# A transformer block on one core: odd halves scaled on ScalarE with an adding transfer, expert tiles in the place of filler transposes, odd gates one term later

## What is computed

```python
x = x + layernorm(attn(layernorm(x)))          # attn(x) = x + ripple(x)
x = x + layernorm(ffn(layernorm(x)))

# ripple: 8 heads of 16; tokens 0,1,2,4,...,512 back
w    = softmax(q . k[t - off] / 4)             # 11 terms
tele = sum_off w[off] * v[t - off]
conv = depthwise causal convolution of v, 7 taps
low  = (fq @ (fk^T v)) / (fq . sum fk)         # fq, fk = elu(.) + 1
out  = (tele + conv + low) @ Wo

# ffn: 8 experts of 64 hidden units, top 2 of them, and one shared expert
scores = sigmoid(x @ gate_W) * route_scale     # top 2, normalised
y = sum_e gate[e] * (gelu(x @ W1[e] + b1[e]) @ W2[e] + b2[e])
y = y + gelu(x @ Ws1 + bs1) @ Ws2 + bs2
```

## Time and profile before

| | |
|---|---|
| median of 3 runs | 289.01 us (288.4 to 289.19) |
| profiled execution | 289.32 us, span of the trace 287.3 us |
| PE busy | 251.7 us, 88% of the span |
| DVE busy | 233.3 us, 81% |
| ACT busy | 194.9 us, 68% |
| POOL busy | 92.9 us, 32% |
| granted TensorE clock, mean | 0.978 |

### The profile page before, as it was taken

One profiled execution on the slowest core, in us unless ns is written; L12 is line 12 of the kernel. 1 busy time (PEld: TensorE's weight loads), 2 busy tenths in 40 slices (PEclk: granted clock), 3 DMA queues, 4 the chain that ended last, 5 costly groups with the idle time before them and its releaser, 6 DMA issues.

```text
span 287.3 us, 4891 instructions
## 1 busy us (share of the span) xinstructions
PE 251.7 (88%) x1670; PEld 179.6 (63%) x1670; DVE 233.3 (81%) x614; ACT 194.9 (68%) x449; POOL 92.9 (32%) x150
## 2 busy tenths in 40 slices
PE   5965995988798889999988999999989799999993
PEld 5422693786644567787645576797636587785383
DVE  6499789478997869789978969789779989957933
ACT  2383466814979957777899956867798655557841
POOL 5920252114374213217092213117043114331003
PEclk9997997999799999999999999999999999999998
DMA  6508999600279984330479973300699955100012
GB/s 199 134 26 240 222 218 196 127 0 2 71 232 234 220 177 84 65 82 2 136 244 215 238 150 73 73 5 0 193 219 219 214 137 109 40 0 1 0 39 73
DMA packets 24258, 35.27 MB, mean 123 GB/s; under 512 B 4053, under 2 KB 17198, under 8 KB 24234
## 3 DMA queue, kind: packets, MB, share of 16 engines
q1 hardware_dynamic: 20346, 21.59, 26.6%
q0 software_dynamic: 3888, 13.37, 25.0%
HBM read 5.07 MB, written 2.10 MB: 25 GB/s over the span
## 4 chain that ended last, share of the span: by engine, by line
PE 50%; ACT 21%; DVE 18%; POOL 5%; issue 4%; POOLq 0%; DVEq 0%; ACTq 0%
PE psH L1413 11%; PE psF L1475 7%; DVE prods L286 7%; PE psY L1515 6%; PE psA L1319 4%; PE psA L1381 4%; ACT xn L610 3%; PE psA L1515 2%; POOL rstd L491 2%; ACT squares L723 2%; ACT xn L730 2%; PE psG L1501 2%; DVE prods L1048 2%; PE psA L1311 2%; PE psH L1410 2%
## 5 line engine op out<-in xcount | busy, mean ns | idle before, releaser
L286 DVE TENSOR_TENSOR prods<-qT,kT 128x1024 f32<-128x1024 f32 (+1 forms) x48 | 50.5, 1109 | 4.4 <-POOL neg_half L454 2.8
L1413 PE MATMUL psH<-ident,prods 128*128 128x128 f32 x324 | 39.9, 273 | 0.0
L491 POOL TENSOR_TENSOR rstd<-var,neg_half 128x4 f32<-128x4 f32 (+2 forms) x27 | 37.2, 1378 | 2.2
L1413 PEld LDWEIGHTS psH<-ident,prods 128*128 128x128 f32 x324 | 36.4, 141 | 2.3 <-issue 2.3
L489 POOL TENSOR_SCALAR var<-ss 128x4 f32<-128x4 f32 (+1 forms) x24 | 8.2, 343 | 90.7 <-ACT squares L778 39.2
L1048 DVE TENSOR_TENSOR prods<-v_shift,prob 128x896 f32<-128x896 f32 x32 | 34.7, 1083 | 0.0
L1475 PE MATMUL psF<-x3T,w 128*128 128x512 f32 x58 | 29.4, 614 | 1.4 <-ACT hid L754 1.4
L1381 PE MATMUL psA<-prods,slot_sel 128*32 128x512 f32 x168 | 24.1, 624 | 5.4 <-DVE kv L988 2.3
L1048 DVE TENSOR_TENSOR prods<-v_tok,prob 128x128 f32<-128x128 f32 (+2 forms) x60 | 20.9, 370 | 3.5 <-PE psH L1413 3.3
L754 ACT ACTIVATE hid<-psF,b1c 128x512 f32<-128x512 f32 x29 | 19.1, 688 | 6.6 <-PE psF L1475 6.6
L1191 DVE TENSOR_TENSOR hid<-hid,psG 128x512 f32<-128x512 f32 x30 | 19.3, 681 | 3.3 <-PE psG L1501 3.3
(11 more groups left out here) (253 smaller groups left out, 591.7 us busy)
## 6 DMA issues: line engine op xcount, KB each, us to landing
v_shift<-v_tok SPq DMA_DIRECT2D x20, 448.0 KB
convT<-tapT POOLq DMA_DIRECT2D x8, 512.0 KB, 6.2
x_res<-L_attn_x SPq DMA_DIRECT2D x4, 512.0 KB, 9.4
tapT<-tapT POOLq DMA_DIRECT2D x4, 512.0 KB, 11.5
out<-y_out SPq DMA_DIRECT2D x7, 256.0 KB, 2.3
x_in<-L_attn_x SPq DMA_DIRECT2D x3, 512.0 KB, 4.1
v_shift<-v_tok SPq DMA_DIRECT2D x4, 384.0 KB
convT<-kexp POOLq DMA_DIRECT2D x3, 512.0 KB, 9.5
```

The lines of the kernel that those rows point to most:

```text
L286: return eng.tensor_tensor(prods[:, QUADS * (s % 2) + q, t0:t1], qT[:, t0:t1], kT[:, PRE - off + t0:PRE - off + t1], ALU.mult)
L491: return nc.gpsimd.tensor_tensor(rstd[:, cols], var[:, cols], neg_half[:, cols], ALU.pow)
L1413: ins = pe.matmul(dst, terms[:, j % TERM_BUFS, m, :], ident[:], is_transpose=True, start=False, stop=(m == live[-1]))
```

## The change

It has these parts, all in passes 1 to 3 (the end in pass 4 keeps its order):

1. Odd units 1 and 3 go the even units' way: `scale_outputs(u0 - 1)` at the start of ACT's pass and `add_residual(u0 - 1)` on POOL, ahead of `ln1`. DVE's `finish` for them goes. `residual` of the odd half waits for the landing of that transfer.
2. All of these units' outputs lie in one bank, `psG[:, 0]`, no longer the even ones in `psY`. PE's waits move with it: `output` and `experts_out` each lose one, and `spread_gates` waits for the scaling.
3. PE: the first two tiles of `experts_out(u0)` stand where 18 filler transposes were, ahead of `turn_x3(u1)` and of the next batch's K projection; the other two stand between the steps of the front of u1; K follows them. The 14 fillers ahead of `output(b, 1)` give way to one tile of u1 (pass 0 keeps them), and the last tile of u1 no longer stands in the next pass. In pass 3 one of two groups of 12 fillers goes.
4. DVE: six gate steps of u0 stand ahead of `residual(u1)`; `weigh_low` follows the second pair of `gate_hidden` (its reciprocal stays ahead); the 24 gate steps of u1 stand in j = 2 to 4, up to three in a place, where they were in j = 1 to 4, two in a place.
5. ACT: the taps come later by one, and tap 6 stands behind `evacuate_x3(u1)`; `normalise3(u1)` stands ahead of the evacuation of the transposed next batch; `norm4` of the odd unit follows fk's evacuation.
6. POOL: of the last two tap additions, that of tap 6 comes last.

```diff
         def outputs(u):
             if u < 2 * B - 3:
-                return psG[:, 0, :] if u % 2 else psY[:]
+                return psG[:, 0, :]
             return psY[:] if u == 2 * B - 1 else psA[:, u % 2, :]
...
             def sum_taps_third(b):
-                pool.wait_ge(tap_scaled, upto(b - 1, TAPS, 7))
                 pool.wait_ge(sums_added, N_DMA * upto(b - 1, N_SUMS, 2))
-                add_tap(b, 0, 6, sums_added)
-                pool.wait_ge(sums_added, N_DMA * upto(b - 1, N_SUMS, 3))
                 pool.wait_ge(side_added, N_DMA * upto(b - 1, N_SIDE, 2))
                 add_tap(b, 0, 2, sums_added)
+                pool.wait_ge(tap_scaled, upto(b - 1, TAPS, 7))
+                pool.wait_ge(sums_added, N_DMA * upto(b - 1, N_SUMS, 3))
+                add_tap(b, 0, 6, sums_added)
...
-                tiles = slice(0, TPH)
-                pool.wait_ge(out_scaled, u // 2 + 1)
-                nc.gpsimd.dma_start(y_out[:, tiles, :], x2[:, tiles, :], accum_op=ALU.add).then_inc(x2_added, N_DMA)
+                tiles = slice(u % 2 * TPH, (u % 2 + 1) * TPH)
+                pool.wait_ge(out_scaled[u % 2], u // 2 + 1)
+                nc.gpsimd.dma_start(y_out[:, tiles, :], x2[:, tiles, :],
+                                    accum_op=ALU.add).then_inc(x2_added[u % 2], N_DMA)
...
                 if attn:
+                    if b >= 2:
+                        ln4(u0 - 1)
+                        add_residual(u0 - 1)
                     if more:
                         ln1(b + 1)
-                    if b >= 2:
-                        ln4(u0 - 1)
...
                 if attn:
+                    if b >= 2:
+                        scale_outputs(u0 - 1)
                     if ffn:
                         gate_logits(u0)
-                        scale_taps(b, range(4, TAPS))
+                        scale_taps(b, range(3, 6))
...
+                    if ffn:
+                        normalise3(u1)
                     if more:
                         evacuate_x(b + 1)
                     if ffn:
-                        normalise3(u1)
                         evacuate_x3(u1)
+                        scale_taps(b, range(6, TAPS))
                         evacuate_shared(u1)
                         gate_logits(u1)
...
                         evacuate_x3(2 * b)
-                        scale_taps(b + 1, range(1, 2))
                         token_major_fk(b + 1)
-                        evacuate_shared(2 * b)
-                        scale_taps(b + 1, range(2, 3))
                         if ffn:
                             norm4(u1)
-                        scale_taps(b + 1, range(3, 4))
+                        evacuate_shared(2 * b)
+                        scale_taps(b + 1, range(1, 3))
...
                 dve.wait_ge(x_res_ld, upto(b, N_DMA, 16))
                 dve.wait_ge(ln2_ready, u + 1)
                 if 0 < b < B - 1 and half:
-                    dve.wait_ge(out_ready[1], upto(b, TPH, 0))
+                    dve.wait_ge(x2_added[1], upto(b, N_DMA, 0))
                 elif 0 < b < B - 1:
-                    dve.wait_ge(x2_added, upto(b, N_DMA, 0))
+                    dve.wait_ge(x2_added[0], upto(b, N_DMA, 0))
...
-                    if b >= 2:
-                        finish(u0 - 1)
                     if ffn:
+                        gates(u0, range(4, 10))
                         residual(u1)
-                        gates(u0, range(4, 24))
+                        gates(u0, range(10, 24))
                     softmax_logits(b)
                     if ffn:
                         gate_hidden(u0, range(0, 2))
-                    weigh_low(b)
+                    invert_low()
                     if ffn:
                         gate_hidden(u0, range(2, 4))
+                    weigh_low(b)
                     softmax_weights(b)
                     for j in range(NT):
-                        def two_gate_steps(n):
-
-                            if ffn and 1 <= j <= TPH:
-                                gates(u1, range(2 * (3 * (j - 1) + n), 2 * (3 * (j - 1) + n + 1)))
-
-                        weigh(b, j, two_gate_steps)
+                        def three_gate_steps(n):
+
+                            if ffn and 2 <= j <= TPH:
+                                first = 3 * (3 * (j - 2) + n)
+                                gates(u1, range(min(first, N_GATE_STEPS), min(first + 3, N_GATE_STEPS)))
+
+                        weigh(b, j, three_gate_steps)
                         if ffn:
...
             def output(b, half):
                 pe.wait_ge(hT_ready, upto(b, 2, half + 1))
-                if b and not half:
-                    pe.wait_ge(out_scaled, b)
...
                     if c == 0 and u % 2 == 0 and 0 < u < 2 * B - 2:
-                        pe.wait_ge(out_ready[1], upto(u // 2, TPH, 0))
+                        pe.wait_ge(out_scaled[1], u // 2)
+                    elif c == 0 and u % 2 and u < 2 * B - 1:
+                        pe.wait_ge(out_scaled[0], u // 2 + 1)
...
             def experts_out(u, tiles=range(TPH)):
                 if u >= 2 * B - 3:
                     pe.wait_ge(scores_read, 2 * B)
-                elif u % 2 == 0:
-                    pe.wait_ge(low_used, u // 2 + 2)
...
                     if ffn:
                         turn_logits(u0)
-                        if b >= 2:
-                            experts_out(u0 - 1, range(TPH - 1, TPH))
...
                     if ffn:
                         spread_gates(u0, range(2, 4))
-                    if more and ffn:
-                        pe.wait_ge(hidden_free, upto(u1, N_HIDDEN, -1))
-                        keep_busy(FILL_K, front(u1, X3))
+                    if ffn:
+                        pe.wait_ge(gated, upto(u0, 4, 4))
+                        experts_out(u0, range(0, 2))
+                        turn_x3(u1)
+                        experts_out(u0, (2,))
+                        gate_logits(u1)
+                        experts_out(u0, (3,))
+                        turn_logits(u1)
                     if more:
                         project_k(b + 1)
-                    else:
-                        keep_busy(FILL_LAST, psA[:, 0, :])
                     if ffn:
-                        turn_x3(u1)
-                        experts_out(u0, (0,))
-                        gate_logits(u1)
-                        experts_out(u0, (1,))
-                        turn_logits(u1)
-                        experts_out(u0, range(2, TPH))
...
                     if more:
                         if ffn:
                             pe.wait_ge(gated, upto(u1, 4, 4))
-                        keep_busy(FILL_OUT, psG[:, 1, :])
+                            experts_out(u1, (0,))
+                        else:
+                            keep_busy(FILL_OUT, psG[:, 1, :])
...
                         project_v(b + 1)
                         if ffn:
-                            experts_out(u1, range(0, 2))
+                            experts_out(u1, range(1, 3))
                         token_major_v(b + 1)
                         turn_x3(2 * b)
                         if ffn:
-                            experts_out(u1, range(2, 3))
+                            experts_out(u1, (3,))
```

More of the change, by code:

```diff
@@ L51 @@
 FILL_FRONT = 5
-FILL_LAST, FILL_K, FILL_OUT = 12, 18, 14
+FILL_LAST, FILL_OUT = 12, 14
 CH = 5
@@ L783, in scale_outputs @@
                 if u >= 2:
-                    act.wait_ge(out_stored[0], upto(u // 2, N_DMA, 0))
+                    act.wait_ge(out_stored[u % 2], upto(u // 2, N_DMA, 0))
                 act.wait_ge(ln4_ready, u + 1)
-                for j in range(TPH):
-                    last = nc.scalar.activation(y_out[:, j, :], outputs(u)[:, bass.ts(j, P)], ACT.Copy,
+                for n, j in enumerate(unit_tiles(u)):
+                    last = nc.scalar.activation(y_out[:, j, :], outputs(u)[:, bass.ts(n, P)], ACT.Copy,
                                                 scale=rstd4[:, j:j + 1])
-                last.then_inc(out_scaled, 1)
+                last.then_inc(out_scaled[u % 2], 1)
             first_normalise()
```

16 lines of the change are left out of this document (8 added, 8 removed).

## The result

The changed kernel takes 291.45 us (median of 9 runs, 290.67 to 293.52), the kernel before 289.17 us (288.17 to 290.48, 9 runs) beside it. The ratio is 1.010, 95% interval 1.007 to 1.013: slower by 0.7 to 1.3%, where 0.9% faster was forecast. The time lies above the predicted range. Some executions took over 1.5% longer than the fastest of the same kernel (295.9 us against 288.68 with the odd half finished on DVE); all medians and ratios here leave them out, and one kernel whose profiled execution was of that kind is left out of the table of lengths.

A forecast was written before the change was run, and what follows sets the result against it. A chain nearly all ACT, then PE until the terms' end, was taken to bound each pass. Terms -1.3 - 0.3 - 1.3 + 0.8 - 0.5 = -2.6 us gave 286.4 us from 289.01; range 283.9 to 289.3 us.

The forecast's parts named there:

- is it kept?: Whether PE's 1.3 us lasts until the terms end: PE stays the bound and passes it on.
- PE's stretch: Passes 1 and 2, from K to the terms' end: hidden of u1 starts earlier, 1.3 us saved in each.
- Pass 2, first norm: ACT's stretch: first norm of batch 3, waiting for `ln1`, starts at 149.2, not 149.5 us: 0.3 us saved.
- Landing: Odd half's adding transfer lands in 5.5 us, bounds 3.3 and 9: nothing lost in pass 2, 0.8 us in pass 3.
- Rival 1: Odd half's landing is slow, deciding point 7.0 us; at 9 us the time is 293.0 us. Chance 0.13.
- Pass 3 after the exponential: Tiles replace fillers; PE could save up to 2 us, DVE allows 0.59 less 0.2: 0.5 us saved.
- The tap sums are also needed at `add_conv`; they have some us of room in pass 1: In PE's stretch, tap sums were taken not to hold up `add_conv`, so the 1.3 us is kept.
- rival 3: PE's 1.3 us given back as taps' sum, Gelu or second gates set `add_conv`: 288.4 us. Chance 0.10.
- if `add_conv` waits for the taps' sum: One of three signs, in the profile after, that would show the prediction wrong.
- rival 4: PE's clock falls; without fillers the new gap is 1.1 us, in pass 3 about 1.4. Chance 0.05.

The follow-up runs named there:

- late taps, old order: Changed kernel with the last two tap additions in their former order and, in pass 3, the first pair issued behind `ln3(u1)`: 288.36 us, ratio 0.999.
- gap filled: Kernel of "late taps, old order" plus 16 PE fillers in pass 3 where PE waits for the odd half's landing: 286.09 us, ratio 0.9919.
- fastest version: Kernel of "late taps, old order" with the odd half finished on VectorE, no odd adding transfer: 286.1 us, ratio 0.9905; run again 285.54 us, 0.9892.
- late taps alone: Changed kernel with only the first pair of tap additions of pass 3 moved behind `ln3(u1)` on POOL: 291.2 us, ratio 1.0089.

## Why the prediction was wrong

The working of single steps held; the question "is it kept?" did not.

- **PE's stretch**, forecast 1.3 us saved each pass: 1.47 us in pass 1 (41.37 to 39.90 in all kernels with the old tap order) and in pass 2 of the changed kernel (41.39 to 39.92, with `add_conv` waiting for PE). Right.
- **Pass 2, first norm**, forecast 0.3 saved: against the start of the half it began at 19.65 us and not 20.03 (147.42 - 127.77; 149.50 - 129.47), 0.4 saved. Right. `ln1` took 3.0 us, forecast 3.2. The squares behind the norm then waited 0.93 us for the landing, which I had at nothing, so the odd half as a whole lost 0.67 us.
- **Landing**, taken as 5.5 us: 6.11 and 5.7 us. Pass 3's odd half lost 1.06 us, forecast 0.8. Right. Rival 1 (slow landing, from 7.0 us on) didn't come.
- **Pass 3 after the exponential**, forecast 0.5 saved: 38.2 us in the versions in which nothing else stood in the way, against 38.94, 0.75 saved. The size was right for what I costed, and the changed kernel still lost 3.73 us there: 1.2 us up to `add_conv` (29.1 us behind the squares against 28.0) and 2.6 us from there to the last norm (13.5 against 11.0). This term is off by 4.2 us, more than all the others together.

The step that failed first, in the order of time, is the sentence "The tap sums are also needed at `add_conv`; they have some us of room in pass 1", and with it rival 3's chance of 0.10. I priced the landing of single sums and not the new order of waits: `convT<-fkT`, which had run beside the side sum, now stood behind it. The rows were there: the four sums' issues in the trace of before, and the lines of the diff. It took 1.2 us in pass 1 of the changed kernel (0.8 to 1.2 in four profiles, nothing in two) and nothing in its pass 2. Where the sums start late, it took 6.1 us in pass 3 (44.25 against 38.18): 3.3 us until `add_conv` and 2.8 us behind it, where the clock was down (0.50 from 240 to 246 us). The forecast had named its sign ("if `add_conv` waits for the taps' sum").

The second, where most of the time went, is in "Pass 3 after the exponential": DVE's small wait of 0.59 us was taken for the only limit. `v_shift` was no term of the sum. In the trace of before its last issue is at 218.51 us, and DVE's first term at 228.95 has no wait. I read "no wait" as "has room". That trace does not show the landing; with the 10.83 us that the last one took in the changed kernel it would be at 229.3 us, an estimate that leaves no room at all. The engines were full: before, their share is 0.97 to 1.04 from 210 to 234 us. Here an earlier start of everything brought nothing forward (last issue 218.08 us after a first one 2.5 us sooner), and holding back the sums did. SP's `v_shift` needed 19.1 us from first to last issue beside POOL's sums in the changed kernel, and 13.7 us when these were held back (late taps, old order). I had counted such crowding for the landing of one transfer only.

The third is rival 4, the clock, chance 0.05. What a fall costs there, on which its share of the range and of the chances rests, was an estimate of mine that no run shows; the runs showed 2.6 and 1.6 us longer stretches with a fall in them. It came in two shapes: behind DVE's late terms (0.50 for a stretch of 4 us; the 2.6 us behind `add_conv` above) and, in another version, behind PE's wait for the landing (0.58, 1.6 us up to `add_conv`). I had looked for new gaps only where fillers went, and not where PE, with less to do, would wait for others.

These three do not add; in pass 3 all of them end in the same place, DVE's terms and `add_conv`, so that where one goes another can take over (I read this off the traces; no run shows it by itself). One edit alone gave 0.1 to 0.75% and two gave 1.1%. Three gave 0.8% with the fillers at the term tiles as the third, 1.8% with the gap filled, and 2.0%, from 1.010 to 0.990, in the fastest version. With the transfer kept, the gap filled, the taps late and in their old order, the time is 0.9919 of before, 2.3 us saved, against 2.6 forecast.

Left open: why the odd half of pass 2 takes 21.5 to 22.8 us with the transfer (without it, it takes 22.1, as ScalarE's squares wait 1.37 us for `residual` behind `finish`), and how often each version meets a clock fall of some 0.7 us in the rest of pass 2 (39.9 us, or 40.6 with a granted clock of 0.57 to 0.71 in one stretch of 4 us from 150 to 158 us; 41.5 in one version without a fall); single profiled executions do not tell. Nor is it shown why the late taps alone gained next to nothing on the changed kernel.

## What to carry over

A resource can be full without a wait that shows: before, the share of the DMA engines was near 1.0 for 24 us, and DVE's first term at 228.95 us had no idle time. Before counting on an earlier start, look for the full one and ask what each transfer in it is needed for, and when: delay the one with the later deadline. Where the diff swaps two waits of a serial chain, write the chain out with its durations, both ways. And where an engine gets less work, it gets new gaps: price the clock in those too (here a term tile took 2.35 us at 0.50 and 1.22 us at 250.80 us).

## What the runs showed of the hardware

Adding transfers took more of the engines' time per byte than SP's transfers, which are copies for the most part, beside them. The page's queue rows for 190 to 256 us of the kernel before (packets, MB, share of 16 engines; q0 is POOL's adding queue, q1 SP's):

```profile
q0 software_dynamic: 1008, 3.41, 28.1%
q1 hardware_dynamic: 3246, 4.65, 25.3%
```

That is 8.2% per MB against 5.4%, half as much again; the two differ in packet size too, 3.4 against 1.4 KB, so that the adding alone is not shown to be the cause. In the changed kernel the granted clock goes to 0.50 after stretches of 4 us in which PE was busy 2.4 and 2.0 us, and its mean was still 0.87 in the stretch from 246 us, although PE was busy in all of it. A gap does not always bring a fall: in the version with the gap filled PE was busy 2.0 us from 236 to 240 us, and the clock stayed at 1.00.
